# Three graph-attention layers on one core: TensorE's segment sums moved ahead of the next chunk's gather

## The chip, the cores and the metric
One core of a Trainium2 chip. The metric is the device time of the whole program in microseconds (us), lower is better: the median of several executions without the profiler. TensorE is written PE, VectorE DVE, ScalarE ACT, GpSimd POOL, and SP is the engine that issues the plain DMAs.

## What is computed
The reference runs L = 3 transformer-convolution layers over N = 6250 nodes and 206250 edges sorted by destination `dst`, with D = 64 features. For each layer:

```
q, k, v = x@Wq+bq, x@Wk+bk, x@Wv+bv;  e = edge_attr@We
alpha = sum(q[dst] * (k[src] + e), -1) / sqrt(D)
p = exp(alpha - segment_max(alpha, dst)[dst])
w = p / segment_sum(p, dst)[dst]
x' = relu(segment_sum((v[src] + e) * w, dst) + x@Ws + bs)
```

After the first two layers comes a layer norm with gamma and beta. After the third come a log-softmax, the addition of the program's input x and a last layer norm.

The kernel keeps the algebra in node space. U = x @ (Wq Wk', Wq We', ...) is one row of 129 numbers for each node (`UC`), with which alpha of an edge is the dot product of U[dst] and [x[src], edge_attr, 1]. The weighted sums of [x[src], edge_attr, 1] by destination are taken first, and Wv and We are applied to these afterwards.

## The kernel before
**Tiling.** The edges are cut into C = 124 chunks of 1664 (T = 13 tiles of 128 edges). Because they are sorted, the destinations of a chunk lie in a window of 64 node rows (`W`) that begins at the chunk's first destination. There are four slots of buffers (`SLOTS`); a chunk uses slot s = chunk mod 4. Each layer walks its 124 chunks in order, so there are 372 chunk steps. Neighbouring chunks may share their boundary node, whose running sum and running maximum are handed on through `old` and merged by DVE at `merge` (L804, semaphore `merged`). A general path for other inputs exists and doesn't run here.

**What a chunk needs.** POOL issues 13 indirect DMAs (`gather`, L442) that fetch x[src] into `feat[s]`; for chunk c+4 they wait until chunk c is merged (L452). SP loads the edge attributes (L297) and two copies of the window's rows of U (`u_win`, L311), also behind `merged`, and stores the finished rows. At a layer's end POOL waits for `layer_stored`.

**The steps of one chunk**, with the number that the code counts them by (n1 for chunk c, so n + 2 is the chunk one ahead and n + 3 the chunk two ahead, n the chunk before):

- DVE `node_mask` (L692, L694) builds the mask `ne` of edge against window row. PE `turn_mask` (L972) transposes it in 7 matmuls into bank 5 of `u_ps`. ACT `mask_rows` (L479, L481, each twice) turns that into the one-hot matrix `mT`, of which there is one buffer.
- ACT `u_high` (L487), DVE `u_remainder` (L700), ACT `u_middle` (L492, L493), DVE `u_last` (L705) split the window's U into three bf16 parts in `u_parts`, also one buffer.
- PE `gather_u` (L981, L982) multiplies `mT` by the parts: 26 bf16 matmuls that write U[dst] of all 13 tiles into `u_ps`.
- DVE `scores` (L715) takes the 13 dot products with `feat`, `maxima` (L722, L725) masks them and takes the maximum per window row.
- PE `turn_max` (L988), DVE L826 to L835, PE `spread_max` (L992): the maximum is transposed, joined with the one handed on, and spread to all partitions. DVE `subtract_max` (L729), ACT `exponentials` (L505): `prob`.
- PE `sums` (L998): 13 float32 products `prob' feat` accumulate in `agg_ps`; the profile has two records for each, 26 in all. ACT `copy_sums` (L497) takes them to `state`, DVE `merge` adds the boundary row.
- Node work on the chunk before: PE `turn_sums` (L1002), `node_product` (L1006), DVE `node_inverse`, `node_out`, `node_norm`, and in the first two layers PE `node_rows` (L1012, L1014), which makes the next layer's U.

**The order of the work** is written out by hand for each engine. ACT in a chunk (L545 to L567): `copy_sums` of the chunk before, `old`, `aggT`, `factor`, `exponentials`, `node_std`; then it waits for `u_gathered` n + 2 and does `u_high`, `mask_rows` and `u_middle` of the chunk two ahead, and last `node_copies`. DVE (L807 to L844): `scores`, `u_last` of the next chunk, `idx` (L817), `maxima`, `merge` of the chunk before, the joined maximum, `subtract_max`, `node_out`, `node_mask` and `u_remainder` for the chunk two ahead, `node_norm`. `u_remainder` waits for ACT's `u_high`, `u_last` for ACT's `u_middle`. In the third layer `node_final` (L797) of an older chunk stands between `u_last` and `idx`.

PE's order is that of `chunk` at L1017, which the change touches:

Of the kernel before, what the change touches and what calls it, by code (L numbers as in the profile page):

```python
# [54 lines left out]
def gnn_kernel(nc, x, xT, src, dst, edge, w_qT, w_ke, w_sk, w_ve, w_vec, out, x_table, u_table):  # L55
    with ExitStack() as ctx:
# [6 lines left out]
        def sem(name):  # L63
            return ctx.enter_context(nc.semaphore(name))
# [171 lines left out]
        xo_ready = sem("xo_ready")  # L236
# [27 lines left out]
        pe_mark = sem("pe_mark")  # L264
# [677 lines left out]
        def _(pe):  # L942
# [24 lines left out]
            def turn_mask(k, n1):  # L967

                pe.wait_ge(ne_ready, n1)
                for t in range(0, T, 2):  # L970
                    w = min(2, T - t) * W
                    ins = nc.tensor.transpose(neT_ps[0:w, t // 2, :], ne[k][:, t:t + w // W, :].rearrange("p t n -> p (t n)"),  # L972
                                              ident_b[:])
                ins.then_inc(neT_done, 1)

            def gather_u(n1):

                pe.wait_ge(mT_ready, n1)
                pe.wait_ge(parts_ready, n1)
                for t in range(T):  # L980
                    nc.tensor.matmul(u_slot(t), mT[:, t, :], u_parts[:, 0:UC], start=True, stop=False)  # L981
                    ins = nc.tensor.matmul(u_slot(t), mT[:, t, :], u_parts[:, UC:2 * UC], start=False, stop=True)  # L982
                ins.then_inc(u_gathered, 1)

            def turn_max(n1):
                pe.wait_ge(cmax_ready, n1)
                pe.sem_inc(pe_mark, 1)
                nc.tensor.transpose(cmT, cmax[:], ident[:]).then_inc(cmT_done, 1)  # L988

            def spread_max(n1):  # L990
                pe.wait_ge(diag_ready, n1)
                nc.tensor.matmul(m_bc, ones[0:W, :], diag[:], start=True, stop=True).then_inc(m_bc_done, 1)  # L992

            def sums(s, n1):

                pe.wait_ge(prob_ready, n1)
                for t in range(T):
                    ins = nc.tensor.matmul(agg, prob[:, t, :], feat[s][:, t, 0:UC], start=(t == 0), stop=(t == T - 1))  # L998
                ins.then_inc(agg_done, 1)

            def turn_sums(k):
                nc.tensor.transpose(aggT_ps, state[k][0:W, 0:F2], ident[0:W, 0:W]).then_inc(aggT_done, 1)  # L1002

            def node_product(n1):
                pe.wait_ge(aggT_ready, n1)
                nc.tensor.matmul(o_ps, aggT[:], ve_cur[:], start=True, stop=True).then_inc(o_done, 1)  # L1006

            def node_rows(s, n1):

                pe.wait_ge(xnew_ready, n1)  # L1010
                pe.sem_inc(pe_mark, 1)
                nc.tensor.transpose(xnT_ps, xnew[s][:], ident[0:W, 0:W]).then_inc(xnT_done, 1)  # L1012
                pe.wait_ge(xnT_ready, n1)
                nc.tensor.matmul(uo_ps, xnT[:], g_next[:], start=True, stop=True).then_inc(uo_done, 1)  # L1014


            def chunk(l, c, s, last, before, more, more2):  # L1017
                n = pe.snap(l * C + c)
                n1 = pe.snap(n + 1)
                k = s % 2  # L1020
                turn_max(n1)
                if before:
                    pe.wait_ge(merged, n)
                    pe.sem_inc(pe_mark, 1)
                    turn_sums(1 - k)
                pe.wait_ge(sel_ready, n1)
                pe.sem_inc(pe_mark, 1)
                nc.tensor.matmul(old_ps, sel[:], state[1 - k][:], start=True, stop=True).then_inc(old_done, 1)  # L1028
                spread_max(n1)
                if before:  # L1030
                    node_product(n)
                if more:
                    gather_u(n + 2)
                if more2:
                    turn_mask(k, n + 3)
                if before:
                    pe.wait_ge(xo_ready, n)
                    pe.sem_inc(pe_mark, 1)
                sums(s, n1)
                if before and not last:  # L1040
                    node_rows((s - 1) % SLOTS, n)
                    pe.wait_ge(uo_ready, n)
                    pe.sem_inc(pe_mark, 1)

            def sorted_layer(l, last):
                pe.wait_ge(ne_ready, l * C + 2)
                pe.sem_inc(pe_mark, 1)
                turn_mask(0, l * C + 1)
                gather_u(l * C + 1)
                turn_mask(1, l * C + 2)  # L1050
                pe.wait_ge(layer_w, l + 1)
                pe.sem_inc(pe_mark, 1)
                for s in range(SLOTS):
                    chunk(l, s, s, last, s > 0, True, True)
                with pe.Fori(1, GROUPS - 1) as g:
                    for s in range(SLOTS):
                        chunk(l, g * SLOTS + s, s, last, True, True, True)
                for s in range(SLOTS):
                    chunk(l, C - SLOTS + s, s, last, True, s < SLOTS - 1, s < SLOTS - 2)
                n = pe.snap(l * C + C)  # L1060
                pe.wait_ge(merged, n)
                pe.sem_inc(pe_mark, 1)
                turn_sums(1)
                node_product(n)
                if not last:
                    node_rows(SLOTS - 1, n)
                    pe.wait_ge(uo_ready, n)
# [79 lines left out]
```

## Time and profile before

| | us |
|---|---|
| median of 3 timed runs | 6415.17 |
| lowest, highest | 6414.19, 6416.32 |
| span of the profiled execution | 10221.2 |
| busy in it: PE | 4680.2 |
| busy: POOL | 4568.1 |
| busy: DVE | 4304.9 |
| busy: ACT | 2615.5 |

The profiled execution has no time of its own beside its span. That span is 1.59 times the median, so this profile can't be read as a scaled picture of a timed run: durations of single instructions can be used, while the idle stretches have to be judged one by one. In the tables of the trace a line gives start and duration in us, the engine, the source line, the operation, output <- inputs, shapes, a count where like instructions are merged, and in square brackets the idle time before it with what ended it ("remote": nothing that the profile can name; "issue": the engine waited for nothing that it shows). `PEclk` is the granted clock of PE: 0.50 is 1.2 GHz, 1.00 is 2.4 GHz.

### The profile page before, as it was taken

The numbers are of one execution on the slowest core, as the hardware profiler recorded it, in microseconds if no ns is written. First come the engines' busy times: TensorE is split into PE (matmuls) and PEld (weight loads), VectorE is DVE, ScalarE is ACT, GpSimd is POOL, SyncE is SP. The second block draws the span as 40 slices with busy tenths as digits, with TensorE's granted clock in tenths as the row PEclk, the third lists the DMA queues.
The fourth block names the chain that finished last, engine by engine and source line by source line (L and its number), as shares of the span: only waits on it lengthen the run. The fifth ranks groups of instructions, "written<-read, shape, count | busy, mean of one in ns | idle before, by whom it ended". The sixth has DMA issues, their size and how long they took to land.

```text
span 10221.2 us, 104558 instructions
## 1 busy us (share of the span) xinstructions
PE 4680.2 (46%) x25782; PEld 3119.1 (31%) x25782; DVE 4304.9 (42%) x19388; ACT 2615.5 (26%) x6114; POOL 4568.1 (45%) x4842
## 2 busy tenths in 40 slices
PE   4444444444444444444444444434444444444444
PEld 3332333333333223332333333322222323232233
DVE  3444444444444344444444444434444444444444
ACT  2222222222222222222222222222222222222222
POOL 4444444444444444444444444444444444444443
PEclk8666666666666666666666666665666565666656
DMA  3111111111111111111111111111111111111111
GB/s 83 36 39 36 39 37 39 37 39 37 37 38 36 35 37 39 37 39 37 39 37 39 37 39 37 38 34 35 37 36 35 35 38 35 35 38 36 35 37 29
DMA packets 906731, 387.54 MB, mean 38 GB/s; under 512 B 758448, under 2 KB 828848, under 8 KB 906544
## 3 DMA queue, kind: packets, MB, share of 16 engines
q1 hardware_dynamic: 751920, 228.08, 9.8%
q0 software_dynamic: 154752, 158.78, 8.1%
q8 instruction: 25, 0.41, 0.0%
q14 instruction: 34, 0.28, 0.0%
HBM read 362.94 MB, written 26.89 MB: 38 GB/s over the span
## 4 chain that ended last, share of the span: by engine, by line
another core or an unknown queue 51%; ACT 18%; DVE 15%; issue 10%; PE 6%; DVEq 0%; DMA 0%; ACTq 0%; SPq 0%
DVE cmax L725 6%; ACT mT L479 5%; ACT mT L481 5%; DVE score L722 3%; ACT prob L505 2%; PE agg_ps L1028 2%; DVE dot_out L715 2%; PE max_ps L988 1%; PE agg_ps L1002 1%; ACT u_mid L493 1%; ACT u_parts L492 1%; ACT lnv L514 1%; PE max_ps L992 1%; DVE score L729 1%
## 5 line engine op out<-in xcount | busy, mean ns | idle before, releaser
L442 POOL DMA_INDIRECT feat<-x_table,idx x3224 | 3041.5, 943 | 3762.5 <-DVE state L804 2744.0
L998 PE MATMUL agg_ps<-feat,prob 128*64 128x129 f32 x9672 | 2145.4, 328 | 2474.4 <-issue 2454.1
L442 POOL DMA_INDIRECT feat<-x,idx x1612 | 1526.0, 947 | 1835.7 <-DVE state L804 1372.8
L998 PEld LDWEIGHTS agg_ps<-feat,prob 128*64 128x64 f32 x9672 | 1340.9, 162 | 3068.3 <-issue 3058.2
L700 DVE TENSOR_TENSOR u_rest<-u_win,u_parts 128x129 f32<-128x129 f32 x372 | 110.0, 296 | 4581.4 <-ACT u_parts L487 2721.2
L487 ACT CAST u_parts<-u_win 128x129 bf16<-128x129 f32 x372 | 112.7, 303 | 4639.4 <-remote 4503.6
L715 DVE CUSTOM_DVE_ANT_0 dot_out<-feat,u_ps 128x129 bf16<-128x129 f32 x4836 | 1044.7, 285 | 84.3 <-issue 80.7
L981 PE MATMUL u_ps<-u_parts,mT 128*128 128x129 bf16 x4836 | 1069.7, 312 | 19.8 <-ACT mT L481 19.8
L982 PE MATMUL u_ps<-u_parts,mT 128*128 128x129 bf16 x4836 | 1076.8, 314 | 0.0
L988 PE MATMUL max_ps<-ident,cmax 128*64 128x128 f32 x372 | 145.3, 391 | 1520.4 <-DVE cmax L725 1520.4
L479 ACT ACTIVATE mT<-u_ps 64x896 bf16<-64x896 bf16 x744 | 675.7, 908 | 550.5 <-remote 542.4
L981 PEld LDWEIGHTS u_ps<-u_parts,mT 128*128 128x128 bf16 x4836 | 699.9, 146 | 63.6 <-ACT mT L481 20.4
L982 PEld LDWEIGHTS u_ps<-u_parts,mT 128*128 128x128 bf16 x4836 | 716.8, 148 | 0.0
L1014 PE MATMUL max_ps<-g_next,xnT 65*64 65x193 f32 x496 | 222.2, 550 | 905.6 <-ACT xnT L533 905.6
L481 ACT ACTIVATE mT<-u_ps 64x768 bf16<-64x768 bf16 x744 | 599.8, 806 | 8.8
L725 DVE TENSOR_REDUCE cmax<-score 128x64 f32<-128x832 f32 x372 | 574.9, 1545 | 12.9
L988 PEld LDWEIGHTS max_ps<-ident,cmax 128*64 128x64 f32 x372 | 47.6, 128 | 1736.8 <-issue 1736.8
L729 DVE TENSOR_TENSOR score<-score,max_ps 128x832 f32<-128x832 f32 x372 | 379.8, 1021 | 241.9 <-PE max_ps L992 241.2
L505 ACT ACTIVATE prob<-score 128x832 f32<-128x832 f32 x372 | 333.7, 897 | 570.1 <-issue 415.7
L715 DVE DVE_READ_ACCUMULATOR2_ANT alpha<- 128x1 f32 x4836 | 401.3, 83 | 27.2 <-issue 26.3
L992 PE MATMUL max_ps<-diag,ones 64*128 64x64 f32 x744 | 254.3, 444 | 330.9 <-DVE diag L834 224.1
L551 ACT COPY old<-agg_ps 1x130 f32<-1x130 f32 x372 | 95.6, 257 | 1150.1 <-PE agg_ps L1028 1150.1
(108 smaller groups left out, 5092.1 us busy)
## 6 DMA issues: line engine op xcount, KB each, us to landing
feat<-edge SPq DMA_DIRECT2D x372, 416.0 KB
feat<-x_table,idx POOLq DMA_INDIRECT x3224
u_win<-u_table SPq DMA_DIRECT2D x744, 48.2 KB
feat<-x,idx POOLq DMA_INDIRECT x1612
u_table<-u_out SPq DMA_DIRECT2D x248, 48.2 KB
u_table<-big SPq DMA_DIRECT2D x13, 386.0 KB
x_table<-xnew SPq DMA_DIRECT2D x248, 16.0 KB
x_table<-x SPq DMA_DIRECT2D x2, 1664.0 KB
```

Source lines behind the costliest of these rows:

```text
L442: nc.gpsimd.indirect_dma_start(feat[s][:, t, 0:D], None, table, bass.IndirectOffsetOnAxis(idx[s][:, t:t + 1], 0),).then_inc(rows_loaded[s] ...
L479: nc.scalar.activation(mT_by[half, 0, 0:(T + 1) // 2, :], neT_ps[0:W, 0:(T + 1) // 2, :], ACT.Copy, scale=-1.0, bias=1.0)
L481: ins = nc.scalar.activation(mT_by[half, 1, 0:T // 2, :], neT_ps[W:P, 0:T // 2, :], ACT.Copy, scale=-1.0, bias=1.0)
L505: nc.scalar.activation(prob[:], score[:], ACT.Exp).then_inc(prob_ready, 1)
L715: ins = nc.vector.tensor_tensor_reduce(dot_out[:, t, :], feat[s][:, t, 0:UC], u_slot(t), 1.0, 0.0, ALU.mult, ALU.add, alpha[:, t:t + 1])
L722: nc.vector.scalar_tensor_tensor(score[:], ne[k][:], -BIG, alpha[:].unsqueeze(2).to_broadcast([P, T, W]), ALU.mult, ALU.add).then_inc(scor ...
L725: nc.vector.tensor_reduce(cmax[:], score[:].rearrange("p t n -> p n t"), AX.X, ALU.max).then_inc(cmax_ready, 1)
L729: nc.vector.tensor_tensor(score[:], score[:], m_bc.unsqueeze(1).to_broadcast([P, T, W]), ALU.subtract).then_inc(shifted, 1)
L981: nc.tensor.matmul(u_slot(t), mT[:, t, :], u_parts[:, 0:UC], start=True, stop=False)
L982: ins = nc.tensor.matmul(u_slot(t), mT[:, t, :], u_parts[:, UC:2 * UC], start=False, stop=True)
L992: nc.tensor.matmul(m_bc, ones[0:W, :], diag[:], start=True, stop=True).then_inc(m_bc_done, 1)
L998: ins = nc.tensor.matmul(agg, prob[:, t, :], feat[s][:, t, 0:UC], start=(t == 0), stop=(t == T - 1))
```

## The change
In PE's order for a chunk, the wait for `xo_ready` and `sums` go ahead of `gather_u` and `turn_mask`. Nothing else is touched; no other engine's order changes, and every instruction is still issued once.

```diff
                 spread_max(n1)
                 if before:
                     node_product(n)
+                if before:
+                    pe.wait_ge(xo_ready, n)
+                    pe.sem_inc(pe_mark, 1)
+                sums(s, n1)
                 if more:
                     gather_u(n + 2)
                 if more2:
                     turn_mask(k, n + 3)
-                if before:
-                    pe.wait_ge(xo_ready, n)
-                    pe.sem_inc(pe_mark, 1)
-                sums(s, n1)
                 if before and not last:
                     node_rows((s - 1) % SLOTS, n)
                     pe.wait_ge(uo_ready, n)
```

## Rows read from the trace of the kernel before
**Rows 1.** The page, its first line.
```profile
span 10221.2 us, 104558 instructions
```
**Rows 2.** Waits: engine, line, releaser: us in total, times, longest us.
```profile
ACT u_parts L487 <- remote: 4503.6, 351, 45.1
POOL feat L442 <- DVE state L804: 4116.8, 360, 52.1
...
DVE state L804 <- ACT state L497: 15.4, 3, 6.6
```
**Rows 3.** Timeline of a steady chunk step in the second layer, all engines.
```profile
5014.23 0.91 ACT L479 ACTIVATE mT<-u_ps 64x896 bf16<-64x896 bf16 x1 [1.19 <-remote]
...
5023.48 0.69 PE L992 MATMUL max_ps<-diag,ones 64*128 64x64 f32 x2 [0.88 <-DVE diag L834]
...
5037.30 0.94 POOL L442 DMA_INDIRECT feat<-x_table,idx  x1 [0.30 <-issue]
...
5038.16 0.30 ACT L487 CAST u_parts<-u_win 128x129 bf16<-128x129 f32 x1 [11.24 <-remote]
```
**Rows 4.** Timeline of PE, the last three chunks of the first layer.
```profile
3375.17 0.69 PE L992 MATMUL max_ps<-diag,ones 64*128 64x64 f32 x2 [0.88 <-DVE diag L834]
...
3389.14 0.69 PE L992 MATMUL max_ps<-diag,ones 64*128 64x64 f32 x2 [0.93 <-DVE diag L834]
...
3400.76 0.43 PE L992 MATMUL max_ps<-diag,ones 64*128 64x64 f32 x2 [0.88 <-DVE diag L834]
```
**Rows 5.** Timeline of POOL: the first layer's fifth chunk, the second layer's first four.
```profile
131.66 0.94 POOL L442 DMA_INDIRECT feat<-x,idx  x1 [52.06 <-DVE state L804]
...
3417.70 0.94 POOL L442 DMA_INDIRECT feat<-x_table,idx  x1 [54.79 <-SPq L338]
...
3481.36 0.94 POOL L442 DMA_INDIRECT feat<-x_table,idx  x1 [0.30 <-issue]
```
**Rows 6.** Timeline of the program's start: a gather beside a two-input DVE operation.
```profile
15.78 1.84 DVE L671 TENSOR_TENSOR wide<-far,lim 128x1612 f32<-128x1612 f32 x1
...
16.87 1.56 POOL L442 DMA_INDIRECT feat<-x,idx  x1 [0.30 <-issue]
```
**Rows 7.** Groups by line: busy us, mean ns of one, idle us before it.
```profile
L722 DVE SCALAR_TENSOR_TENSOR score<-ne,alpha 128x832 f32<-128x832 bf16 x372 | 375.4, 1009 | 1.2 <-issue 1.1
```
**Rows 8.** Timeline of the first chunk step, before any of the long idle stretches.
```profile
118.95 0.69 PE L992 MATMUL max_ps<-diag,ones 64*128 64x64 f32 x2 [0.88 <-DVE diag L834]
...
119.56 0.29 PE L981 MATMUL u_ps<-u_parts,mT 128*128 128x129 bf16 x1
...
120.72 0.90 ACT L505 ACTIVATE prob<-score 128x832 f32<-128x832 f32 x1 [1.53 <-DVE score L729]
...
122.36 1.09 PE L972 MATMUL u_ps<-ident_b,ne 128*128 128x128 bf16 x7
...
123.48 0.91 ACT L479 ACTIVATE mT<-u_ps 64x896 bf16<-64x896 bf16 x1 [0.53 <-PE u_ps L972]
```
**Rows 9.** Timeline of PE: two whole `sums`, around the layer's end and start.
```profile
3403.23 5.85 PE L998 MATMUL agg_ps<-feat,prob 128*64 128x129 f32 x26 [1.78 <-ACT prob L505]
...
3504.61 3.04 PE L998 MATMUL agg_ps<-feat,prob 128*64 128x129 f32 x26
```
**Rows 10.** Windows, PE: length, busy (instructions), granted clock, DMA share, GB/s.
```profile
3403.00:3409.00 6.00, 5.77 (x26) 0.50 0.02 3
...
5024.00:5027.00 3.00, 3.00 (x27) 0.50 0.42 69
5027.00:5028.20 1.20, 0.80 (x12) 1.00 1.11 252
...
133.00:139.00 6.00, 6.00 (x45) 0.50 0.56 115
```
**Rows 11.** Timeline of a chunk step in the third layer, ACT and PE.
```profile
9017.51 0.91 ACT L479 ACTIVATE mT<-u_ps 64x896 bf16<-64x896 bf16 x1
...
9027.20 0.69 PE L992 MATMUL max_ps<-diag,ones 64*128 64x64 f32 x2 [0.88 <-issue]
```

## The prediction
> **What bounds the kernel now.** I read the page first, for its span against the median: 10221 us profiled [rows 1], 6415.17 us timed. Over 372 chunk steps that is about 27 us a step with the profiler and 17 without, so some 10 us a step are in the profile alone and must be found and taken out. The waits say where [rows 2]: ACT waited 4504 us at `u_high` for something "remote", and POOL 4117 us for the merge. The timeline of a steady step shows the first: ACT's `u_high` starts at 5038.16 after 11.24 us idle [rows 3], though PE's gather of U, which it waits for, began right behind `spread_max` at 5024.2 and needs 2.8 us (below). PE's work is there, its completion comes late. Where POOL isn't gathering, this doesn't occur: in the first steps [rows 8] and at the end of the first layer [rows 4]. There one step, `spread_max` end to `spread_max` end, takes 3389.83 - 3375.86 = 13.97 us, node work included. Were the late completion real in a timed run, no step could take 17 us. I take it as the profiler's.
>
> So the chain of compute takes about 14 us. The other candidate is POOL. Its 52 gathers at the start of the second layer stand back to back: (3481.36 - 3417.70) / 51 = 1.248 us each [rows 5], 16.23 us for 13. That exceeds 14, so in a timed run POOL never sleeps and sets the pace, while the chain of compute waits for its rows. One thing more slows POOL: a gather that begins at 16.87 inside a DVE operation with two inputs in SBUF takes 1.56 us instead of 0.94, and is over 0.81 us after that operation's end at 17.62 [rows 6]. In the steady steps of the profile the masked scores (L722, 1.009 us, two SBUF inputs [rows 7]) fall just ahead of the merge, where POOL sleeps; in a timed run POOL doesn't, and they collide. A gather that meets it at a random moment loses 1.009 x 1.009 / (2 x 1.248) = 0.41 us on average a step; seven shorter two-input operations add between nothing and 0.25. So POOL needs 16.64 to 16.89 us a chunk; I take 16.84.
>
> The page "SBUF — State Buffer" of the Trainium skill (section "Who interferes with whom") says that a DVE instruction with two SBUF inputs contends with a GpSimd instruction that reads SBUF, and that one blocks until the other is done. By that rule the 0.41 us belongs in the sum, and the trace agrees: 1.56 against 0.94.
>
> **The sum against the median.** Layer 1: POOL resumes at 131.66 [rows 5], then 120 x 16.84 = 2021; from the last gather to the last `spread_max` about 8.5 (an estimate: 2 for landing, four dot products, the maxima and the 2.9 us behind them); from there to the next layer's first gather 3417.70 - 3401.19 = 16.5 [rows 4, 5]. Together 2178. Layers 2 and 3: 124 x 16.84 + 25 = 2113 each. Sum 6404, which is 11 under the median. Without the DVE term it would be about 6180. The stalls taken out, the trace and the median agree within 0.2%, and I keep the 11 as an offset.
>
> **The change, part by part.** (1) Removed: nothing. (2) Added: nothing; the wait on `xo_ready` moves with `sums` and is over about 1 us before `prob` is, so it costs nothing; without that cover it would still be the same wait. (3) Moved: `sums`, 26 records, from behind the gather of U and the mask to ahead of them. It must wait for `prob`, so PE, which filled that wait with the gather, now stands idle in it. Behind it are queued the gather (26 matmuls) and the mask (7), and on them wait ACT's `u_high` and `mask_rows`, behind these DVE's `u_remainder` (with `node_norm` and `scores` behind it) and `u_last`. No DMA and no queue of SP or POOL is passed; SP's stores come later with `xnew`, which nothing in the next step waits for.
>
> The new step, counted from `spread_max` end:
>
> - `prob` is ready 121.62 - 119.64 = 1.98 us later, and 0.05 until the first matmul [rows 8].
> - `sums`: 5.85 us at the granted clock 0.50, 3.04 at twice that rate [rows 9, 10]. PE has been idle, so it starts low. After dense work begins behind an idle stretch the clock was up 3 us later in one place, and in another still low after 6 [rows 10]. With 4 us low, then high: 4.9 us. Ends: 3.04 and 5.85.
> - Gather of U: 122.36 - 119.56 = 2.80 us low [rows 8]; by the ratio of the two `sums`, 1.4 high. Taken mostly high: 1.6.
> - Mask and hand-over to ACT: 123.48 - 122.36 = 1.12 low [rows 8]. High about 0.8; the mask itself is long ready. 0.8.
> - From ACT's first `mask_rows` to `spread_max` end: 5024.17 - 5014.23 = 9.94 us [rows 3]: four ACT copies, the U split, `u_last`, maxima, the joined maximum. Unchanged. `scores` runs beside the ACT copies, about 0.5 us short of them, so the later gather doesn't add there.
>
> Sum 1.98 + 0.05 + 4.9 + 1.6 + 0.8 + 9.94 = 19.3 us, against the 16.84 of POOL, which now sleeps. The chain of compute becomes the bound; only the first 2.5 us of its growth hide in POOL's lead. With everything low the step is 21.7, with everything high 17.2. In the third layer the same stretch of 9.94 is 9027.89 - 9017.51 = 10.38, so 0.44 more [rows 11].
>
> Total: layer 1: 119.6 + 123 x 19.3 + 16.5 = 2510. Layer 2: 25 + 123 x 19.3 + 16.5 = 2415. Layer 3: 2415 + 123 x 0.44 = 2469. Sum 7394, with the offset 7405; I say **7400 us**, 15% slower. One us a step is 369 us.
>
> What the move should gain is nothing: `sums` is copied and merged only behind the next chunk's maxima, and the merge waited 15.4 us in the whole trace for the copy [rows 2].
>
> **Rivals.** A, **it hides**: PE stays at the high clock, the step is 17.2 us or a little less, and POOL's pace covers nearly all. Total 6415 to 7405 - 369 x 2.1 = 6630. For it: the burst is now longer and in one piece. Against: 1.98 us idle before it, more small waits around the maximum, and dense work behind an idle stretch always started low in the rows that I read. Chance 0.08.
>
> B, **PE is slowed in timed runs too** while POOL gathers, by part of what the profile shows; then the step before is bound by compute at about 16.9 us, not by POOL, with 2.7 us more than my 14.2, and the change adds its full 5.1: 22.0 us, 7405 + 369 x 2.7 = 8400. For it: the "remote" wait of rows 3 ends at 5038.16, within 0.1 us of the end of POOL's 13th gather (5038.24), so the stalls do follow POOL. Against: POOL's own rows already explain the median to 0.2%. Chance 0.09. The same page of the skill says that PE and ACT never wait on anyone for SBUF; by that rule the stall isn't contention for SBUF, which takes some chance from B.
>
> C, **faster**: in timed runs the merge does wait for the sums' copy, and POOL sleeps for the merge; then the median's 235 us over POOL's bare pace (6415 - 6180) is that sleep, and earlier sums take it away: 6180. It decides if the copy ends behind the maxima. Against: 15.4 us of wait in 372 merges [rows 2], and ACT copies the sums only behind `node_copies`, which the change makes later. Chance 0.02. A smaller mishap, that ACT or DVE work that I hold parallel lines up, lies in the range.
>
> **The numbers.** Forecast (step 18.2 to 20.6 us) 0.81, A 0.08, B 0.09, C 0.02. The range for 8 in 10: 7000 (step 18.2, early rise of the clock) to 7900 (step 20.6, late rise or 1 us more of waits); A, B and C are left out, 0.19. A measurement of this kernel can tell about 0.2% from no change. Faster by more: C, 0.02. Within: a part of A, 0.03. Slower: 0.95.
>
> **What would show it.** In the profile after: `sums` starts about 2 us behind `spread_max` with PE idle before it, released by `prob` instead of following the mask; `u_high` and `u_remainder` start behind `sums`; from the first `mask_rows` to `spread_max` still 9.9 us. The profiler's stalls will now fall partly inside `sums`, ahead of the gather, and its span will be 10200 to 11200 us, again no scaled picture. At the undisturbed places (first steps, the second chunk of layer 2) the step should read 18 to 21 us where about 14 stand now. Wrong would be: that step under 17, or POOL without idle time in a version whose PE isn't stalled, or a median above 8000.

## The result, and the profile after
The new order takes **7449.79 us** (median of 4 runs, 7448.72 to 7450.61) against 6415.74 for the kernel before: ratio 1.161, 95% interval 1.159 to 1.163. The forecast was 7400 us, range 7000 to 7900, slower with a chance of 0.95.

One fact has to come first, since no number below can be read without it: the timed runs come in two regimes, all runs made together in the same one, and by its medians the kernel before takes 6416 to 6425 us in the first, which is that of the result, and 10147 to 10246 us in the second. The profile of the kernel before, on which the prediction rests, belongs by its span to the second, and the profile after to the first. So no trace here shows the kernel before in the first regime, and what it did there is concluded from its times and from variants. Ratios are taken only within one regime.

The page of the changed kernel, first lines and the two groups that answer to the question. Columns of a group: busy us, mean ns of one, idle us before it and what ended it.

```profile
span 7447.4 us, 104558 instructions
...
PE 3974.8 (53%) x25782; PEld 3192.5 (43%) x25782; DVE 4308.3 (58%) x19388; ACT 2631.5 (35%) x6114; POOL 4647.6 (62%) x4842
...
PE 48%; ACT 25%; DVE 22%; issue 4%; DVEq 0%; DMA 0%; POOL 0%; SPq 0%; ACTq 0%; POOLq 0%
...
L998 PE MATMUL agg_ps<-feat,prob 128*64 128x129 f32 x9672 | 2014.5, 401 | 610.5 <-ACT prob L505 566.3
```

The span fits the timed runs: the profiled execution took 7449.38 us. The chain that ended last now has names: PE 48%, over half of it the segment sums (27% of the span on the page). In front of these PE stands idle 610 us in all and is released by `prob`, where before they followed the mask. Next the waits (us in total, times, longest). [Rows 2] have the same waits for the order before, but in the second regime, so their sizes can't be compared with these.

```profile
ACT u_parts L487 <- PE u_ps L982: 2342.3, 369, 7.5
DVE u_rest L700 <- ACT u_parts L487: 2256.1, 372, 17.8
...
POOL feat L442 <- DVE state L804: 1246.4, 345, 13.7
```

ACT waits for the gather of U behind the sums, 6.3 us a step, DVE for ACT. POOL waits for the merge before 345 of its gathers, 3.6 us each time on average, so it doesn't set the pace. A step of the second layer in the timeline:

```profile
3000.04 0.68 PE L992 MATMUL max_ps<-diag,ones 64*128 64x64 f32 x2 [0.88 <-DVE diag L834]
...
3001.82 0.90 ACT L505 ACTIVATE prob<-score 128x832 f32<-128x832 f32 x1 [1.53 <-DVE score L729]
...
3002.76 5.83 PE L998 MATMUL agg_ps<-feat,prob 128*64 128x129 f32 x26 [1.64 <-ACT prob L505]
...
3008.53 0.23 PE L981 MATMUL u_ps<-u_parts,mT 128*128 128x129 bf16 x1
...
3010.06 0.67 PE L972 MATMUL u_ps<-ident_b,ne 128*128 128x128 bf16 x7
...
3010.77 0.91 ACT L479 ACTIVATE mT<-u_ps 64x896 bf16<-64x896 bf16 x1 [0.21 <-PE u_ps L972]
...
3020.02 0.68 PE L992 MATMUL max_ps<-diag,ones 64*128 64x64 f32 x2 [0.88 <-DVE diag L834]
```

Read as terms, each up to the start of the next: 2.04 us until the sums, 5.77 for them, 1.53 for the gather, 0.71 for mask and hand-over, 9.93 from the first `mask_rows` to the next `spread_max` end. In the two first layers three steps repeat, with sums of 5.83, 4.41 and 5.35 us; the clock in the windows (length, busy, granted clock, DMA share, GB/s) of the first of them, over its sums and over the gather behind:

```profile
3002.80:3008.50 5.70, 5.70 (x26) 0.50 0.43 97
3008.50:3010.00 1.50, 1.50 (x27) 1.00 0.09 22
```

The first and last `spread_max` of the first layer, and of the third:

```profile
75.72 0.68 PE L992 MATMUL max_ps<-diag,ones 64*128 64x64 f32 x2 [0.89 <-DVE diag L834]
...
2455.30 0.68 PE L992 MATMUL max_ps<-diag,ones 64*128 64x64 f32 x2 [0.88 <-DVE diag L834]
...
4915.21 0.69 PE L992 MATMUL max_ps<-diag,ones 64*128 64x64 f32 x2 [0.88 <-DVE diag L834]
...
7431.42 0.68 PE L992 MATMUL max_ps<-diag,ones 64*128 64x64 f32 x2 [0.88 <-DVE diag L834]
```

(2455.30 - 75.72) / 123 = 19.35 us a step, (7431.42 - 4915.21) / 123 = 20.46.

### The profile page after: what moved, and what is told of

Its sections match the earlier page's. It is cut to its first block, busy times and chain, and to the rows that moved or that the text cites. A ratio compares the mean times of both kernels' runs of the same rounds, so it can differ in the third digit from the quotient of the medians.

```text
span 7447.4 us, 104558 instructions
## 1 busy us (share of the span) xinstructions
PE 3974.8 (53%) x25782; PEld 3192.5 (43%) x25782; DVE 4308.3 (58%) x19388; ACT 2631.5 (35%) x6114; POOL 4647.6 (62%) x4842
## 4 chain that ended last, share of the span: by engine, by line
PE 48%; ACT 25%; DVE 22%; issue 4%; DVEq 0%; DMA 0%; POOL 0%; SPq 0%; ACTq 0%; POOLq 0%
PE agg_ps L998 27%; ACT mT L479 8%; DVE cmax L725 8%; ACT mT L481 7%; DVE score L729 5%; DVE score L722 5%; PE u_ps L981 4%; ACT prob L505 4%; PE u_ps L982 4%; PE max_ps L992 3%; PE agg_ps L1028 3%; PE u_ps L972 2%; PE max_ps L988 2%; PE agg_ps L1002 1%; ACT u_mid L493 1%
## 5 line engine op out<-in xcount | busy, mean ns | idle before, releaser
L442 POOL DMA_INDIRECT feat<-x_table,idx x3224 | 3085.3, 957 | 1887.9 <-issue 913.8
L998 PE MATMUL agg_ps<-feat,prob 128*64 128x129 f32 x9672 | 2014.5, 401 | 610.5 <-ACT prob L505 566.3
L998 PEld LDWEIGHTS agg_ps<-feat,prob 128*64 128x64 f32 x9672 | 1895.3, 216 | 680.1 <-ACT prob L505 630.8
L442 POOL DMA_INDIRECT feat<-x,idx x1612 | 1561.7, 969 | 851.1 <-issue 454.6
L715 DVE CUSTOM_DVE_ANT_0 dot_out<-feat,u_ps 128x129 bf16<-128x129 f32 x4836 | 1039.3, 286 | 73.1 <-issue 48.1
L981 PE MATMUL u_ps<-u_parts,mT 128*128 128x129 bf16 x4836 | 609.9, 221 | 19.5 <-ACT mT L481 19.5
L982 PE MATMUL u_ps<-u_parts,mT 128*128 128x129 bf16 x4836 | 607.1, 224 | 0.0
L981 PEld LDWEIGHTS u_ps<-u_parts,mT 128*128 128x128 bf16 x4836 | 472.3, 99 | 112.8 <-issue 92.7
L982 PEld LDWEIGHTS u_ps<-u_parts,mT 128*128 128x128 bf16 x4836 | 471.1, 97 | 0.0
L992 PE MATMUL max_ps<-diag,ones 64*128 64x64 f32 x744 | 254.2, 444 | 331.1 <-DVE diag L834 331.1
L1014 PEld LDWEIGHTS max_ps<-g_next,xnT 65*64 65x64 f32 x496 | 64.6, 183 | 839.6 <-ACT xnT L533 839.6
```

The lines of the kernel that those rows point to most:

```text
L442: nc.gpsimd.indirect_dma_start(feat[s][:, t, 0:D], None, table, bass.IndirectOffsetOnAxis(idx[s][:, t:t + 1], 0),).then_inc(rows_loaded[s] ...
L715: ins = nc.vector.tensor_tensor_reduce(dot_out[:, t, :], feat[s][:, t, 0:UC], u_slot(t), 1.0, 0.0, ALU.mult, ALU.add, alpha[:, t:t + 1])
```

## The experiments
**again: the kernel before, profiled once more.**

> The kernel before, unchanged, profiled a second time. The question is whether the 10 us a step by which its first profile exceeds the timed runs belong to the kernel or to one profiled execution. Theory (PE's late completions are an effect of the profiler, tied to this order of work): the timed run is 6415 us again and the span again near 10200 us, with u_high waiting over 10 us for something remote. Rival (that profiled execution was odd): the span is near 6410 us, the step 16.8 us, and POOL has no idle time.

It took 10142 us, and 13 timed runs of the kernel before beside it a median of 10147. So neither of the two: the span is near 10200 us again, but so are the timed runs. The late completions are not the profiler's; they belong to the second regime, in which the runs without the profiler are as long.

**few_old and few_new: one gather of 13 left out.** Each order with

```diff
-                for t in range(T):
+                for t in range(T - 1):
                     nc.gpsimd.indirect_dma_start(
```

the thirteenth source tile set to ones once, and DVE's wait for the rows set to one gather fewer.

> The order of before, with POOL fetching 12 tiles of x[src] a chunk instead of 13 (the thirteenth tile of the source features is left out and holds ones). Theory (POOL sets the pace of the kernel before): POOL needs 1.25 us a chunk less, 368 x 1.25 = 460 us, so about 5955 us. Rival B (compute bound already, at about 16.9 us a step): no change, 6415 us.

> The same thirteenth gather left out, in the new order. Theory (the chain of compute bounds the new order, POOL sleeps about 3 us a step): no change from 7450 us, within 0.5%. If POOL's pace still mattered there it would fall by up to 460 us.

Both ran in the second regime: 9636 us for the old order, 510 less than the kernel before (ratio 0.949, 0.948 to 0.951), and 9845 for the new. The new order with all 13 gathers didn't run beside them; by its ratio of 1.021 from another group of runs (below) it would take about 10357 us there, an estimate, and that is again about 510 more. That is 1.37 us a step in both orders, a little more than the 1.25 us of one gather. So in the second regime the whole time of one gather lies in series with compute in both orders; that all 13 do is not shown. Of the first regime, for which they were meant, they say nothing.

**new_again and half: the new order, and only the mask moved, in the second regime too.** half is, against the kernel before,

```diff
                     gather_u(n + 2)
-                if more2:
-                    turn_mask(k, n + 3)
                 if before:
                     pe.wait_ge(xo_ready, n)
                     pe.sem_inc(pe_mark, 1)
                 sums(s, n1)
+                if more2:
+                    turn_mask(k, n + 3)
```

> The new order, unchanged, beside the kernel before on the same chip. The last four kernels and the kernel before ran at about 10150 us on another chip than the one of the first comparison, with late completions of TensorE in every timed run. So two regimes exist. If this chip is of the kind that gave 6415 us: 7450 us against 6415, ratio 1.16, steps of 19.3 us. If it is of the kind that gave 10147 us, where TensorE is held up while POOL gathers: the order then matters in another way; by theory both orders wait for the end of POOL's 13 gathers (16.2 us) and then have the same 10 us left until the merge, so the ratio is between 1.00 and 1.08.

> Half of the move: the gather of U stays ahead of the sums, only the turned mask goes behind them (gather, sums, mask). Theory, on a chip of the 6415 us kind: the gather fills the wait for prob, the sums end about 2.9 + 4.6 us after the maximum is spread, the mask 0.8 later, then 9.9 us: a step of about 18.3 us, 7030 us. If only the idle wait ahead of the sums cost, the time would be 6415; if the place of the mask alone didn't matter, 7450. On a chip of the 10147 us kind: near 10150 us.

10445.92 us against 10235.28, ratio 1.021 (1.019 to 1.022), within the 1.00 to 1.08 expected; and 10377.03 for half, ratio 1.014 (1.012 to 1.016), where I had said about no change. The timeline of PE and the release of ACT in new_again, behind a `spread_max` that ended at 5018.76:

```profile
5026.58 0.22 PE L982 MATMUL u_ps<-u_parts,mT 128*128 128x129 bf16 x1
5027.05 0.22 PE L981 MATMUL u_ps<-u_parts,mT 128*128 128x129 bf16 x1 [0.24 <-issue]
...
5029.20 0.22 PE L982 MATMUL u_ps<-u_parts,mT 128*128 128x129 bf16 x1 [1.16 <-issue]
...
5034.16 0.27 PE L972 MATMUL u_ps<-ident_b,ne 128*128 128x128 bf16 x1 [1.02 <-issue]
```

```profile
5035.84 0.30 ACT L487 CAST u_parts<-u_win 128x129 bf16<-128x129 f32 x1 [14.34 <-remote]
```

Its sums began at 5020.81 and took 4.73 us. After about 6 us of dense work PE issues mostly one to three instructions each 1.4 us, with nothing that it waits for in the profile, and ACT starts 4 us behind the gather's last matmul at 5031.34. The stall now falls on the gather and the mask instead of the sums; POOL's gathers began at 5016.92 and ended at 5032.84. The move costs only 0.6 us a step there, but not because the stall is the same: the old order takes 26.6 us a step in [rows 1]'s trace and the new one 27.2, against 14.15 and 19.33 us for the same chains without gathers (below, in the first regime), so 12.5 us come on top in one and 7.9 in the other. In nine of ten steps of new_again ACT's `u_high` starts 2.8 to 3.2 us behind the end of POOL's thirteenth gather, as if the new order went by POOL's gathers and a fixed rest. In the trace of the kernel before the same distance lies anywhere from -3.0 to 2.9 us, so the 0.1 us that the prediction read in one step was chance.

**np_old, np_new, np_half, np_warm: no gathers by POOL at all.** The order before, the new one, the half one, and the new one with dummy matmuls in the idle wait, each with all 13 gathers left out, DVE's waits for their rows too, and the source features set to ones:

```diff
-                for t in range(T):
-                    nc.gpsimd.indirect_dma_start(
-                        feat[s][:, t, 0:D], None, table, bass.IndirectOffsetOnAxis(idx[s][:, t:t + 1], 0),
-                    ).then_inc(rows_loaded[s] if t < T_FIRST else rest_loaded[s], 16)
```

np_warm adds, ahead of the wait on `xo_ready`:

```diff
+                for _ in range(16):
+                    nc.tensor.matmul(u_ps[:, 0, 0:P], ident_b[:], ident_b[:], start=True, stop=True)
```

> The order of before with all of POOL's gathers left out (the source features hold ones, computed from nothing). This takes away both POOL's pace and whatever holds TensorE up while POOL gathers, so that the chain of compute stands alone on any chip. Theory (chain of compute 14.1 us a step): 369 x 14.1 + about 170 at the edges = 5370 us. Rival B (compute itself 16.8 us a step): 6370 us. If the late completions come from the profiler and not from POOL, they stay and the time is over 9500 us.

> The new order, all of POOL's gathers left out. Theory: steps of 19.35 us as in the trace of the changed kernel, 369 x 19.35 + 170 + 100 (longer steps in the third layer) = 7400 us, so 2000 us above the old order without gathers, twice the 1034 us between the two with gathers, since POOL's pace no longer covers the first 2.7 us of each step. If the move costs in another way (through POOL), the distance shrinks below 1034 us.

> Gather of U, then the sums, then the turned mask, all of POOL's gathers left out. Theory: the gather fills the wait for prob, the clock rises earlier since the dense work begins earlier, the mask is turned about 4 us later than in the old order: steps of 17.1 us, 6480 us. If the move of the gather, and not that of the mask, is what costs: 5370 us. If the mask's place is all: 7400 us.

> The new order with 16 dummy matmuls (identity by identity, into a free U bank, overwritten later) in TensorE's idle wait for prob, all of POOL's gathers left out. Theory (the sums run at the low clock because TensorE stands idle before them): the clock rises earlier within the sums, which get up to 0.8 us shorter; steps near 18.8 us, 7110 us. If the idle wait has no part in the clock: 7400 us as without the dummies; if they delay the sums they show as an added 0.3 us or more a step.

These ran in the first regime, beside a kernel before of 6424.61 us:

| | expected us | measured us | ratio to before | step, layers 1 and 2 |
|---|---|---|---|---|
| np_old | 5370 | 5440.0 | 0.847 (0.844 to 0.849) | 14.15 |
| np_half | 6480 | 6522.68 | 1.015 (1.012 to 1.018) | 17.03 |
| np_warm | 7110 | 7032.89 | 1.095 (1.092 to 1.098) | 18.52 |
| np_new | 7400 | 7440.15 | 1.158 (1.155 to 1.162) | 19.33 |

(The steps are the means between the first and the last `spread_max` end of a layer, us.) Three readings. Without gathers the old order falls by 985 us: its chain of compute alone takes 14.15 us, and the rest of its time came from the gathers. Whether by POOL's pace or because PE is slowed beside them (rival B), np_old alone can't tell, since it takes both away. The second reading can: the new order without gathers takes what it takes with them, 7440 against 7450 us, so in this regime the gathers don't slow the chain. psum_old3 below adds the same for the order before: its sums take 3.27 us on average beside the gathers and np_old's 3.31 without, while POOL doesn't wait. And the move costs 5.18 us a step in layers 1 and 2, 2000 us in all, of which POOL's pace covered half.

The half order splits it: putting the sums ahead of the mask alone costs 2.9 us, moving the gather behind them the other 2.3. Its timeline shows why the first part isn't more, and the windows of PE over the gather and over the sums give the clock:

```profile
2006.52 0.69 PE L986 MATMUL max_ps<-diag,ones 64*128 64x64 f32 x2 [0.88 <-DVE diag L828]
2010.46 3.22 PE L992 MATMUL agg_ps<-feat,prob 128*64 128x129 f32 x26
2013.62 0.68 PE L966 MATMUL u_ps<-ident_b,ne 128*128 128x128 bf16 x7
2023.58 0.68 PE L986 MATMUL max_ps<-diag,ones 64*128 64x64 f32 x2 [0.88 <-DVE diag L828]
```

```profile
2007.50:2010.40 2.90, 2.90 (x27) 0.50 0.36 88
2010.50:2013.60 3.10, 3.10 (x27) 0.95 0.38 84
```

(L986, L992 and L966 are here `spread_max`, `sums` and `turn_mask`.) The gather fills the wait for `prob`, and the sums take 3.22 us, not 5.83: PE did dense work just before them, and the granted clock is 0.95 in them. np_warm confirms it from the other side. The sums of np_new, then of np_warm, in the groups by line (busy us, mean ns, idle us before):

```profile
L992 PE MATMUL agg_ps<-feat,prob 128*64 128x129 f32 x9672 | 2012.2, 401 | 610.4 <-ACT prob L501 610.4
...
L992 PE MATMUL agg_ps<-feat,prob 128*64 128x129 f32 x9672 | 1566.9, 336 | 0.7 <-ACT prob L501 0.7
```

1566.9 / 372 = 4.2 us a step against 2012.2 / 372 = 5.4, and the whole kernel is 407 us faster for 5952 matmuls more. The expected gain was 290. In layers 1 and 2 a step is 0.8 us shorter; the surplus comes from the third layer, where it is 1.7 us shorter (18.76 against 20.44). The sums there take 5.84 us on average without the dummies, near the 5.85 of the low clock, and 4.08 with them.

**psum_old, psum_old2, psum_old3: the dot products in PSUM.** The order of before, with one operand of L722 moved, which is also what the dot products (L715) are accumulated into:

```diff
-        alpha = sb("alpha", [P, T])
+        alpha = u_ps[:, 4, 400:400 + T]
```

> The order of before, with the 13 dot products of a chunk kept in PSUM (a free part of the bank of the last U tile) instead of SBUF, so that the masked scores (L722) have one input in SBUF instead of two. Theory (that operation holds POOL's gathers up by 0.41 us a chunk on average): 368 x 0.41 = 150 us less, about 6265 us. Rival (POOL's period is 16.8 us for another reason): no change, 6415 us.

> The same kernel as psum_old (order of before, the 13 dot products of a chunk in PSUM, so that L722 has one input in SBUF), run again because the first time the chip was of the kind on which TensorE is held up and POOL sleeps, where L722 and the gathers don't meet. On a chip of the 6415 us kind, theory (L722 holds a gather up by 0.41 us a chunk on average): 150 us less, about 6265 us, which would beat both kernels. Rival (POOL's period has another cause): 6415 us. On a chip of the other kind: no change.

> The third try of the dot products in PSUM, for a chip of the 6415 us kind. Theory there: L722 no longer holds gathers up, 150 us less, about 6265 us, and no gather of 1.0 us or more begins within L722. Rival: 6415 us. On a chip of the other kind: no gain, as the first two times (10162 against 10147, 10303 against 10246).

The first two fell in the second regime: 10161.65 against 10146.74 (ratio 1.001), 10303.22 against 10246.42 (1.006, 1.004 to 1.007), no gain. The accumulator reads take longer, 143 ns each in psum_old3 against 83; whether they are the small loss isn't shown. The third fell in the first regime: **6136.55 us against 6423.7, ratio 0.955 (0.954 to 0.957)**, faster than both kernels. The gain is 287 us, 0.77 a step, where 0.41 was expected. POOL and DVE in its timeline:

```profile
2006.16 0.29 DVE L715 CUSTOM_DVE_ANT_0 dot_out<-feat,u_ps 128x129 bf16<-128x129 f32 x1 [1.87 <-DMA feat<-x,idx]
2006.18 0.95 POOL L442 DMA_INDIRECT feat<-x,idx  x1 [0.30 <-issue]
...
2007.43 0.94 POOL L442 DMA_INDIRECT feat<-x,idx  x1 [0.30 <-issue]
2007.44 1.01 DVE L722 SCALAR_TENSOR_TENSOR score<-ne,u_ps 128x832 f32<-128x832 bf16 x1
...
2008.68 0.94 POOL L442 DMA_INDIRECT feat<-x,idx  x1 [0.30 <-issue]
```

POOL doesn't stop, one gather each 1.25 us (its waits for the merge are 10.5 us in the whole trace), its step is 16.23 us in layers 2 and 3, and no gather that begins within L722 lasts 1 us or more. Of all 4836 only 29 do, so the seven shorter two-input operations cost little. The trace also says why my mean was too small. DVE's last four dot products wait for the landing of rows, so in a kernel that POOL paces L722 doesn't meet the gathers at random: in 332 of the 372 steps it begins within 0.25 us of the start of a gather. With the shorter accumulator reads of the kernel before (a dot product each 0.21 us instead of 0.25) it would begin 0.16 us earlier; the starts of this trace, shifted by that, give 0.74 us a step of hold-up. That is an estimate, close to the 0.77 gained. The kernel before itself has no trace in this regime. In the changed kernel, where L722 still has two inputs in SBUF and POOL still gathers beside it in some steps, the collision is in the trace:

```profile
149.42 1.01 DVE L722 SCALAR_TENSOR_TENSOR score<-ne,alpha 128x832 f32<-128x832 bf16 x1
149.52 1.73 POOL L442 DMA_INDIRECT feat<-x,idx  x1 [0.30 <-issue]
```

1.73 us instead of 0.94, over 0.82 us after L722's end at 150.43, as in [rows 6]. An undisturbed gather takes 0.94 us, so the part of it that had to wait for L722 begins about 0.13 us behind its start (an estimate, 0.94 - 0.82 or 0.81). By that count 92 gathers of this trace fall within L722, and they last 0.69 us longer than the others on average.

## Why the prediction was right, and where it wasn't
**The bound before** held: POOL, not compute. np_old shows a chain of 14.15 us, np_new that the gathers don't slow it, psum_old3 that POOL has no pause. Its size, 16.84 us, was too small: the term for L722 was 0.41 and is 0.77 by psum_old3, while of the 0.2 for the seven shorter operations hardly anything is seen in psum_old3. From the difference to psum_old3 the step is about 16.24 + 0.77 = 17.0. That the sum met the median within 0.2% was in part luck: 0.16 us over 368 steps is 59 us too little, and the start was 43 us too long, since the first `spread_max` ends at 76.4 us in the changed kernel and at 77.1 in psum_old3, not at the 119.6 of the second regime [rows 8].

**The reading of the late completions** was the step that failed: "I take it as the profiler's". The timed runs in the second regime have them too. It did no harm because the median that was to be explained came from the first regime, and the durations used for the sum are those of stretches behind or beside the stalls. That was luck too: had the comparison been made in the second regime, 15% would have been 2%.

**The new step**, term by term, forecast and measured in layers 1 and 2: until the sums 2.03 and 2.04; sums 4.9 and 5.2 (mean of 5.83, 4.41 and 5.35); gather 1.6 and 1.5; mask and hand-over 0.8 and 0.7; rest 9.94 and 9.93. Sum 19.3 and 19.35. In the third layer 19.74 was forecast and 20.46 measured: PE's sums take 5.8 us on average there, near the 5.85 of the low clock, which is 0.9 above my 4.9, less the 0.2 of gather and mask.

**The total**: 7405 by the sum, less 43 for the earlier start, plus 0.72 x 123 = 89 for the third layer, plus 12 for 0.05 us in 246 steps, less the 11 of the offset, which was none (the profiled execution's time is 2 us above its span), gives 7452 for 7450.

**The rivals.** A (it hides at the high clock) is out: no step has its sums under 4.41 us, where 3.04 is the high clock; np_warm shows that about 1.1 us a step could be had that way. B (PE slowed beside POOL in the timed runs) was wrong for this regime: it asked for 8400 us, and by np_new the gathers are worth 10 us to the new order in the whole program. It was right in kind for the second, where the order before takes about 10 us a step more and not the 2.7 that I priced. That it isn't contention for SBUF, as the page "SBUF — State Buffer" of the Trainium skill has it of PE, no run here tests; its cause stays open, and so does what sets the regime. The runs show only that it is tied to POOL's gathers: it appears beside them, at places without them steps take 14 us [rows 4], and a gather fewer takes 1.37 us off. C (earlier sums help) is out by the result; in the changed kernel the merge waited 14.8 us in all for the sums' copy.

The page's rule of the shared port (section "Who interferes with whom") did hold in a steady step, not only at the program's start: with two SBUF inputs L722 made the gather at 149.52 take 1.73 us, with one no gather that began within it took 1 us, and the kernel lost 4.5% of its time.

## What to carry to other kernels
Put into an engine's forced wait the work that doesn't depend on what it waits for; putting the waiting work first costs the wait, the later start of everything behind it, and on TensorE the low clock as well (sums of 4.41 to 5.83 us in the new order, 3.22 with the gather ahead of them). Before trusting a profile against a median, check that both come from the same regime: a span of 1.59 times the median is a fact about the chip's runs until shown to be the profiler's. When one engine issues indirect DMAs back to back, look which two-input DVE operations meet them, and at which phase; where a wait ties the two to each other, the collision is not the mean over random moments (here 0.77 us a step instead of 0.41).

## What the runs showed of the hardware that was not expected
- Two regimes of the same program on one core, 6416 to 6425 us and 10147 to 10246 us by the medians, each steady to about 0.2% within runs made together; one chip's number came up in both. In the second PE, after about 6 us of dense work beside POOL's gathers, issues mostly one to three instructions each 1.4 us (new_again), and ACT's start came 4 us behind the last matmul that it waits for. The cause is open.
- DVE's dot products can accumulate straight into PSUM, at 143 instead of 83 ns for the read of the accumulator, and the operation that uses them is as fast (1004 against 1009 ns).
- 16 useless matmuls a step made the kernel without gathers 5.5% faster (7032.89 against 7440.15 us).
